# Attention edges taken as 238 tiles of up to four in-edges per node row, instead of 220 groups of 512 edges

## The reference

```python
# layer 0: h summed over in-edges, by edge_weight        (dense, by adjacency blocks)
# layer 1: twice GATv2, each followed by batch norm and PReLU
h = leaky_relu(xj + xr[dst] + eattr @ We, 0.2)           # xj = xl[src], also a self loop per node
logits = h @ att
ex = exp(logits - segment_max(logits, dst)[dst])
out = segment_sum(xj * ex, dst) / segment_sum(ex, dst)
# layer 2: GAT with 4 heads of 64
e = leaky_relu(a_src[src] + a_dst[dst], 0.2)             # softmax over dst as above, per head
# layer 3: GCN with its weights by degree                 (dense, by adjacency blocks)
```

## Time and profile before

| | |
|---|---|
| median of three runs | 5436.29 us |
| span of the profiled execution | 6476.5 us |
| the profiled execution outside its span | the page has no figure for it |
| three attention loops, in the profile | 1488 + 1495 + 1527 = 4510 us |
| everything else, in the profile | 1966 us |
| granted TensorE clock, mean | 0.948 of full speed |
| busy: PE, DVE, ACT, POOL | 77%, 71%, 51%, 49% |

### The profile page before, as it was taken

The page is one execution under the profiler, slowest core; times in us unless marked ns, Lnnn a source line. Parts: engine busy times, 40 slices in busy tenths (PEclk is TensorE's granted clock), DMA queues, the critical chain, the costliest instruction groups (busy, mean ns, idle before and its releaser), DMA issues. The chain is left out here.

```text
span 6476.5 us, 112764 instructions
## 1 busy us (share of the span) xinstructions
PE 4962.1 (77%) x28202; PEld 3616.4 (56%) x28559; DVE 4612.1 (71%) x17132; ACT 3308.1 (51%) x8567; POOL 3157.0 (49%) x3441
## 2 busy tenths in 40 slices
PE   4999999957777877784777777778377666667799
PEld 2444446835555655562656555556255555555588
DVE  8999993446777777775777677777477777777721
ACT  5888882025555555542555555555255555555520
POOL 2444446625555555532555555563255555555400
PEclk9999999979999999997999999999699999999999
DMA  2233347834444444422444444442233333333264
GB/s 57 62 90 103 114 119 262 308 96 99 105 103 106 105 106 106 107 64 64 104 102 105 104 102 105 105 107 66 65 98 100 101 101 102 101 100 101 74 161 115
DMA packets 606518, 695.46 MB, mean 107 GB/s; under 512 B 243043, under 2 KB 512656, under 8 KB 599802
## 3 DMA queue, kind: packets, MB, share of 16 engines
q0 software_dynamic: 128832, 362.75, 22.4%
q1 hardware_dynamic: 477370, 329.75, 18.5%
HBM read 589.91 MB, written 102.19 MB: 107 GB/s over the span
## 5 line engine op out<-in xcount | busy, mean ns | idle before, releaser
L982 POOL DMA_INDIRECT gath<-table,src_col x880 | 845.4, 961 | 892.0 <-issue 623.6
L982 POOL DMA_INDIRECT h<-table,src_col x880 | 840.7, 955 | 584.4 <-issue 584.4
L1121 PE MATMUL psum<-xr 128*128 x3520 | 1040.5, 398 | 36.1 <-ACT xr L1083 18.8
L1070 ACT CAST rows<-psum 128x128 bf16<-128x128 f32 x440 | 116.7, 265 | 1200.9 <-remote 762.6
L705 DVE SCALAR_TENSOR_TENSOR xr<-xr,gath,psum 128x259 f32<-128x259 f32 x1440 | 685.8, 476 | 27.1 <-PE psum L689 5.7
L1206 POOL DMA_INDIRECT gath<-table,src_col x440 | 423.3, 962 | 498.6 <-issue 335.1
L1121 PEld LDWEIGHTS psum<-xr 128*128 128x128 f32 x3520 | 550.5, 197 | 203.0 <-issue 54.3
L1007 DVE TENSOR_REDUCE seen<-psum 128x1 f32<-128x512 f32 x440 | 303.6, 690 | 496.2 <-PE psum L1132 357.4
L1001 DVE SCALAR_TENSOR_TENSOR zs<-zs,mean 128x256 f32<-128x256 f32 x1760 | 649.6, 423 | 0.0
L1206 POOL DMA_INDIRECT h<-table,src_col x440 | 421.9, 959 | 298.8 <-issue 298.8
L1122 PE MATMUL psum<-We,eaT 128*128 128x256 bf16 x1760 | 489.4, 278 | 0.0
(11 more groups left out here) (330 smaller groups left out, 11867.1 us busy)
## 6 DMA issues: line engine op xcount, KB each, us to landing
locrow<-g_locb SPq DMA_DIRECT2D x660, 128.0 KB
pairs<-xr SPq DMA_DIRECT2D x640, 115.5 KB
xr<-pairs SPq DMA_DIRECT2D x13, 1716.0 KB
gath<-table,src_col POOLq DMA_INDIRECT x1320
h<-table,src_col POOLq DMA_INDIRECT x1320
xr<-pairs SPq DMA_DIRECT2D x25, 832.0 KB
acc<-pairs SPq DMA_DIRECT2D x12, 1716.0 KB
xr<-pairs SPq DMA_DIRECT2D x13, 1584.0 KB
```

What stands on the lines that cost most here:

```text
L982: pool.indirect_dma_start(m.gath[r][:, j, :], None, table, bass.IndirectOffsetOnAxis(m.src_col[r][:, j:j + 1], 0)).then_inc(gathered[r], 16)
L1121: nc.tensor.matmul(zb[q][:, j, :], m.hot[r][:, j, :], blk(m.xr, b, 0, D), start=True, stop=False)
```

## The change

A tile is now 128 virtual rows, each holding up to 4 consecutive in-edges of one node (S = 4); a node of degree d takes ceil(d/4) rows. The number of tiles is fixed by the worst case, NT = 238, so that a loop gathers 952 times in place of 880. A new stage `slot_list` finds, for every row of every tile, its node, its first edge and how many edges are left. `build_matrices` fetches the 4 edges' records with 238 indirect DMAs on GpSimd. `spmm_dense` makes from them the source indices, the linear parts of the logits and a mask, and stores the attributes tile by tile. In the loops a row's destination is a single 128x128 one-hot: it is made by ScalarE, turned once by TensorE, and shared by the 4 edges of a row. The maximum is first taken over the row's 4 slots, and only 128 peaks per head are spread. The source indices stay in SBUF and no list is loaded per tile. All engines run the loops unrolled. Constants that are no longer used go.

```diff
-NG = NW + NB - 1
+S = 4
+NT = ((E + (S - 1) * N) // S + (P - 1) * NB) // P
-def pipelined(eng, stages, blocks=None, total=NG, unroll=U):
+def pipelined(eng, stages, blocks=None, total=NT, unroll=U):
...
+def slot_list(nc, m, a):
+            for b in range(NB):                                    # POOL
+                pool.wait_ge(windows, b + 1)
+                pool.indirect_dma_start(dst[:, b, :], None, a["dst"], ...)
...
+            for b in range(NB):                                    # DVE
+                nc.vector.scalar_tensor_tensor(t["junk"], t["last"], t["nid"][:, b:b + 1], t["ones"], ALU.is_lt, ALU.mult,
+                                               accum_out=t["window"][:, b:b + 1]).then_inc(counted, 1)
+                dve.wait_ge(counted, b + 1)
+                nc.vector.tensor_copy(t["window_i"].bitcast(I32)[:, b:b + 1], t["window"][:, b:b + 1]).then_inc(windows, 1)
+            dve.wait_ge(picked, 16 * NB)
+            ... 25 x scalar_tensor_tensor over 128, about 20 small linked operations
+            for b in range(NB):
+                after(dve, placed, b, 2)                           # PE: 3 matmuls of 238 columns, float32
+                nc.vector.tensor_scalar(t["low_hot"][:, b % 2, :], m.irow[:, :], t["low"][:, col], None, ALU.is_equal)
+                nc.vector.tensor_scalar(t["high_hot"][:, 3 * (b % 2), :], t["tile_no"], t["high"][:, col], None, ALU.is_equal)
+                ... two more of these
+            ... 3 running sums over 238 tiles, about 10 small linked operations
...
 build_matrices, POOL
-            pipelined(pool, [(0, weigh)], None, STEPS // 4, SU // 4)
+            def gather_slots(t4, u, turn, of):
+                for t in range(t4 * NT // (STEPS // 4), (t4 + 1) * NT // (STEPS // 4)):
+                    pool.indirect_dma_start(m.slots[:, t * FIELDS * S:(t + 1) * FIELDS * S], None, a["runs"], ...)
+            straight([(0, weigh), (0, gather_slots)], None, STEPS // 4, SU // 4)
...
 spmm_dense, PE (between the block products, beside it 3 stores per chunk of 32 tiles on SP)
+                for g in range(g0, g1):
+                    for r in (0, 1):
+                        mm = nc.tensor.transpose(m.ps[7][...], fields[:, g * longest:g * longest + k, 1 + r].bitcast(F32), m.ident[:, :])
...
 gatv2_loop, POOL
             def gather(t, u, turn, b):
-                pool.wait_ge(listed[r], 16 * nth(u, turn, RG))
-                after(pool, group_sum, t, RG)
-                pool.sem_inc(begun, 1)
-                for j in range(T):
-                    pool.indirect_dma_start(m.gath[r][:, j, :], None, table, ...)
+                after(pool, tile_sum, t, RG)
+                for k in range(S):
+                    pool.indirect_dma_start(m.gath[t % RG][:, k, :], None, table, ...)
...
 gatv2_loop, the order of the stages (lag, stage)
-            straight([(2, sum_inputs), (2, dot), (3, see), (2, add_linear), (5, add_group), (3, raise_top),
-                            (2, high_part), (3, drop), (2, without_high), (3, set_top), (2, middle_part),
-                            (2, low_part)], ...)               # DVE
-            pipelined(act, [(3, copy_turned), (4, copy_weights), (0, place), (1, mask), (3, exponentials)])
-            pipelined(pe, [(3, turn_parts), (4, flip), (3, show_logits), (1, mix), (4, sum_group)], ...)
+            straight([(6, set_top), (4, sum_inputs), (4, add_linear), (4, dot), (5, see), (8, add_tile), (5, raise_top),
+                      (4, add_logits), (5, drop)], ...)        # DVE
+            straight([(5, spread_peak), (6, lower), (1, copy_hot), (1, mask), (6, exponentials), (6, shrinkage),
+                      (0, measure), (6, weigh), (0, own)])     # ACT
+            straight([(1 + BEHIND, bring), (1, flip), (5, show), (7, sum_tile), (3, mix)], ...)   # PE, BEHIND = 5
...
+            def weigh(t, u, turn, b):                              # ACT
+                for k in range(S):
+                    ins = nc.scalar.mul(m.prob[:, t % 2, k * P:(k + 1) * P], m.own[t % RG], m.ex[t % R][:, k:k + 1])
...
 gat_loop, the order of the stages
+            straight([(3, add_dst), (6, see), (3, leak), (6, raise_top), (8, weigh), (3, bar), (6, drop), (7, sink),
+                      (3, peak), (6, set_top), (9, add_tile), (8, rescale)], ...)                   # DVE
+            straight([(4, copy_rows), (1, copy_hot), (1, mask), (0, measure), (7, shrinkage), (7, exponentials), (0, own),
+                      (8, weigh)])                                 # ACT
+            straight([(7, bring), (4, turn_peaks), (1, flip), (3, mix), (9, sum_tile), (5, show)], ...)  # PE
```

More of the change, by code:

```diff
@@ L136, in load @@
             m.tab[0:1, bass.ds(first, n)], engines=[engine], min_val=0, max_val=NB,
-            skip_runtime_bounds_check_because="the list of groups has blocks 0 to NB only")
+            skip_runtime_bounds_check_because="the list of tiles has blocks 0 to NB only")
         return values
@@ L572, in _, with slot_rooms, take @@
                 link(nc.vector.tensor_scalar(needed, needed, 32, None, ALU.add))
+def slot_rooms(m):
+    xr = m.xr3[:, :, :].rearrange("p b c -> p (b c)").bitcast(F32)
+    t, at = {}, [0]
+    def take(name, *shape, room=xr):
+        size = 1
+        for n in shape:
+            size *= n
+        ap = room[:, at[0]:at[0] + size]
+        at[0] += size
+        t[name] = ap if len(shape) == 1 else ap.rearrange("p (a c) -> p a c", a=shape[0])
+    for name in ("last", "junk", "ones"):
+        take(name, NWIN)
+    take("dst", NB, P)
+    for name in ("before", "upto"):
+        take(name, P)
+    take("low_hot", 2, P)
+    take("high_hot", 6, NT)
+    take("starts", 3, NT)
+    take("running", 3, NT)
+    for name in ("window_i", "first", "degree", "rows", "above", "tiles", "tile0", "high", "low", "q", "w1"):
+        take(name, NB)
+    assert at[0] <= (NB + 1) * 3 * D // 2
+    at[0] = 0
+    take("spread", 7, P, room=m.zs_all[:, :])
+    for name in ("tile_no", "place"):
+        take(name, NT, room=m.zs_all[:, :])
+    for name in ("shift_up", "corner_up", "shift_dn", "corner_dn"):
+        take(name, P, room=m.zs_all[:, :])
+    for name in ("nid", "window"):
+        take(name, NB, room=m.zs_all[:, :])
+    assert at[0] <= 2 * T * (D + 3)
+    return t
@@ L600, in stores_of @@
                     _, values = nc.values_load_multi_w_load_instructions(
-                        t["stores"][r][:, bass.ds(first, n)], engines=[mybir.EngineType.SP], min_val=least, max_val=most,
-                        skip_runtime_bounds_check_because="a step is at most the last one, a place of the ring below its length")
+                        t["stores"][r][:, bass.ds(first, n)], engines=[mybir.EngineType.SP], min_val=least, max_val=most)
                     got.append(values)
@@ L669, in room_of @@
                         flat(t["room_needed"][:, bass.ds(turn * (SU // PAUSE), SU // PAUSE), :]),
[L670 to L671 removed]
+                        engines=[mybir.EngineType.PE], min_val=32, max_val=32 * (NSUB // 4 + 1))
                     for k in range(SU // PAUSE):
@@ L817, in _ @@
+            multiply_blocks(nc, m, pe, arrived, ring, lambda i, hb: tiles[i % ring][:, hb, P:2 * P], used, finished, taken,
+                            between={LISTED + 2 * q: (turn_attributes, q) for q in range(len(pairs_of))})
             pe.wait_ge(counted, 2 * NB)
@@ new lines, in sum_tile @@
+            def sum_tile(t, u, turn, b):
+                pe.wait_ge(weights, t + 1)
+                after(pe, done, t, 2)
+                for k in range(S):
+                    mm = nc.tensor.matmul(sum_ps[t % 2], m.prob[:, t % 2, k * P:(k + 1) * P], m.gath[t % RG][:, k, 0:WA],
+                                          start=(k == 0), stop=(k == S - 1))
+                mm.then_inc(tile_sum, 1)
+            straight([(1 + BEHIND, bring), (1, flip), (5, show), (7, sum_tile), (3, mix)],
+                     blocks_on(nc, m, mybir.EngineType.PE))
```

1060 lines of the change are left out of this document (526 added, 534 removed).

## The result

The changed kernel takes 6124.26 us (median of 4 runs, 6123.49 to 6126.64) where the kernel before takes 5436.53: a ratio of 1.1263, 95% interval 1.1247 to 1.1279. It is 688 us slower. The forecast was slower by 334, at 5770, with a range up to 5920. The sign was right, the size was half. Each time is compared with the kernel before in its own session of runs, since that kernel takes 5437 to 5439 us in three sessions and 6481 in a fourth.

A forecast was written before the change was run, and what follows sets the result against it. Before, GpSimd or TensorE explains the loops' 5.0 us per group; after, GpSimd sets the pace. Loops +239, new stage +111, small parts −12.9, −2.7, −1, +4: +337 on 5436 is 5773, said as 5770 us, range 5330 to 5920.

The forecast's parts named there:

- The excess of the profile: Profile against timed runs: the profile's extra 1040 us all lie in the three loops, 3470 us in a timed run.
- GpSimd sets the pace after: Loops after the change: GpSimd's gathers, with no wait left, set the pace, as all other engines need below 5.0 us.
- The weak step: Loops before: GpSimd's four gathers and TensorE both explain 5.0 us per group; if this step fails, the sign fails.
- The consumers' bound of 4.6 us: Loops after: TensorE, the slowest engine using the gathered rows, needs 4.6 us per GATv2 tile at most.
- the rival of slow consumers: Loops after: consumers stay slower than 5.0 us per tile; 5.2 to 5.7 us give 5910 to 6270 us; chance 0.11.
- the cheaper gather: Rival for the loops: gathers cheaper unprofiled, or TensorE alone set 5.02 us; some 5340 us, faster; chance 0.22.
- 952 x 1.25 = 1190 per loop: Each loop after: 952 gathers on GpSimd at 1.25 us each take 1190 us.
- Stalls of 16, 16 and 23 us at the starts: Start of each loop: the trace's stalls stay; if instruction fetch causes them, 55 us go and the kernel takes about 5715.
- Ends of 24, 24 and 30 us: End of each loop: last steps and the gathers' landing take 24 us in the GATv2 loops, 30 in GAT.
- The new stage at 111 us: The added stage `slot_list`, all on the path: 111 us, between 90 and 130.
- The fetches in `build_matrices` cost 0: 238 GpSimd fetches, 298 us, fit its idle time and cost 0; rival of +95 to +298, chance beyond forecast range 0.04.
- The stage unchanged: `build_matrices` stays at 941 us; the forecast's sum adds 0 for it.

The follow-up runs named there:

- masked: The changed kernel with the bounds checks in `build_matrices` replaced by one AND at each wait: 5875.31 us (ratio 1.0801); in the other session 6707.47 us (1.0352).

## Why the prediction was right and where it was wrong

- **The excess of the profile lies in the loops, which take 3470 us in a timed run: right.** The kernel before with the checks, whose profile is as long as its timed runs, has 1135 + 1135 + 1203 = 3473 in the windows above. The reason I gave (signals late in the profiled execution only) was wrong: in one session the timed runs take 6481.41 us, so the profile of 6476.5 was most likely taken in that condition. What the condition is stays open. The late signals are real in it. There `masked` shows an instruction of ScalarE 4.2 us behind the product that it waits for; in the session with 5439.48 the same instruction comes 0.1 us behind the product (third row), which ended at 2003.37:

```profile
2001.06 0.31 PE L1236 MATMUL psum<-ident,xr 128*128 128x128 f32 x1
2005.59 0.17 ACT L1208 ACTIVATE under<-psum 128x1 f32<-128x1 f32 x1 [4.30 <-remote]
2003.46 0.17 ACT L1208 ACTIVATE under<-psum 128x1 f32<-128x1 f32 x1 [0.17 <-PE psum L1236]
```

- **GpSimd sets the pace after: right.** The GATv2 loops have 952 gathers each without a wait. The weak step, two engines that both explain 5.0 us, turned out as "both". The consumers' bound of 4.6 us was 4.40, so the rival of slow consumers is refuted where the kernel before takes 5437, and so is the cheaper gather. In the session with 6481.41 the slow consumers are what happens: a loop of `masked` takes 1505 to 1608 us, over 6.3 per tile. One slip of the working: the starts and ends in the sums of the cheaper gather add up to 139 us, not 131; no verdict hangs on the 8 us.
- **952 x 1.25 = 1190 per loop: mis-sized.** It is 1218 in the first two loops (2972.94 + 0.95 - 1755.4) and 1225 in the third. I used the median, 0.946; the mean is 0.976, and a count of 952 multiplies the mean. +28, +28, +35, where 13 of the last are the waits among the empty tiles.
- **Stalls of 16, 16 and 23 us at the starts: failed.** They are in the earlier trace rows and went with the condition of that profile; neither the changed kernel nor the kernel before with the checks has them: -55. The latter still runs TensorE and ScalarE as hardware loops, so straight code isn't what removed them. By the rule of the Trainium skill ("Runtime: NRT & Kernel Launch", Instruction fetch mechanics) I had 55 us for them; its sum came out, but not for its reason. In the session with 6481.41 `masked`, straight code throughout, still has waits of 8.5, 7.7 and 19.1 us there, where the kernel before with three gathers has 14.0, 15.0 and 23.4; what part the branches have in these is open.
- **Ends of 24, 24 and 30 us: failed, by two errors of opposite sign.** With different rows the ends are 13, 14 and 24; with the one row 50, 50 and 42. That 238 is a worst case, 21 tiles are empty and all their rows the same one, could be read from the code: +64 over what I had.
- **The new stage at 111 us: right**, 108. The 25 fetches started at 83.8 and ended at 119.3, 1.4 us each, where I had 1.3.
- **The fetches in `build_matrices` cost 0: right.** 951 us with them and 951 without, both with the AND. GpSimd's idle time before its turns covered them.
- **The stage unchanged: failed.** This is the step that put the forecast out of its range. The sum takes 0 for `build_matrices` and prices only the fetches there: the list of what the change does read the GpSimd part of the stage and not the loads on SyncE and TensorE. The prediction's own rule, that a full VectorE (912.84 of 941) lets nothing run faster, says nothing on what an added wait can do. The checks are +260 of the 354 us by which the forecast was short. The loops' 101 (91 gathers, 64 ends, -55 stalls) are nearly all of the rest.

## What to carry to other kernels

Price every edit of a diff on every queue, and look first at those that seem to be of safety only: a check of loaded values held SyncE for some 4.1 us per 16 values, and TensorE waited for the stores behind it. Where two engines explain the same pace, relieving one brings nothing, and a run with one gather less tells it. When work is padded to a worst case, ask what the padding does: here 21 of 238 tiles cost some 141 us per loop, a fourth of it because all of them read one row. Before a sum is made, ask whether the profile and the timed runs were taken in the same condition.

## What the runs showed of the hardware

- The same kernel takes 5439 us in one session and 6481 in another, and the ratio of two kernels goes with it: `masked` is 1.0801 of the kernel before in the one, 1.0352 in the other, where ScalarE starts 4.2 us behind a product of TensorE that it waits for. Why is open; both sessions bear chip number 13. With three gathers per group this lateness was mostly gone in the kernel before (5642.78 against 6481.41, and 5448.20 in the other session), but the changed kernel kept 500 us of it (5782.45 against 5282.43).
- 128 descriptors that read one address: DMA engines 99% busy at 83 GB/s, against 42% at 109 GB/s for rows spread over the table; a tile's four gathers then take 6.7 us.
- A check of one loaded value costs SyncE 0.147 + 0.018 us of instructions; 16 of them put some 4.1 us between the end of one load and the start of the next (4.5 in the first turn).
- TensorE's granted clock was 0.99 in `build_matrices` before and without the checks, and 0.86 with them, where TensorE stands still for 285 us in place of 84. Its products became longer (501 ns against 415 for the largest group), and its busy time in the stage is 916 us in place of 867. How much of the 250 us between the two stages comes by this was not separated.
- A gather of GpSimd is 0.946 us in the median and 0.976 in the mean in the changed GATv2 loops, in single cases up to 1.2, and 1.48 in GAT. The rule of the Trainium skill on VectorE's two-port copies ("SBUF — State Buffer", Who interferes with whom) had given up to 121 us for the loops; the lengthening is 78 us in all. In the first two loops the copy isn't what lies beside the long gathers: of 57 of them between 2000 and 2300 us of the changed kernel not one overlaps it.
